# First attention: the value projection of two heads at once, in three rounded passes of 256 columns

## The reference, cut to what matters

```
q = split_heads(x @ Wq);  k = split_heads(x @ Wk);  v = split_heads(x @ Wv)
q = _apply_rope(q, cos, sin);  k = _apply_rope(k, cos, sin)
scores = einsum('bhqd,bhkd->bhqk', q, k) * scale     # causal mask, softmax
ctx = einsum('bhqk,bhkd->bhqd', attn, v)
return ctx.reshape(b, s, H * HD) @ Wo
```

## Time and profile before

| | before |
|---|---|
| median of 3 runs (1079.26 to 1084.4) | 1079.3 us |
| profiled execution: its time / its span | 1087.43 us / 1085.1 us |
| PE busy over the span | 992.0 us (91%) |
| first attention (scores of head 0 to the last mix) | 20 us to 266 us |
| DVE, ACT, POOL busy over the span | 66%, 56%, 44% |

### The profile page before, as it was taken

The page is one execution under the profiler, slowest core; times in us unless marked ns, Lnnn a source line. Parts: engine busy times, 40 slices in busy tenths (PEclk is TensorE's granted clock), DMA queues, the critical chain, the costliest instruction groups (busy, mean ns, idle before and its releaser), DMA issues. The chain is left out here.

```text
span 1085.1 us, 19309 instructions
## 1 busy us (share of the span) xinstructions
PE 992.0 (91%) x6228; PEld 822.2 (76%) x6228; DVE 720.6 (66%) x2139; ACT 606.7 (56%) x1647; POOL 480.1 (44%) x479
## 2 busy tenths in 40 slices
PE   7999999998996799849999999988878889999996
PEld 5998899887883689827888898975435568777785
DVE  5666766664587356528586757646787457888876
ACT  3656665666222355437676777637774565555553
POOL 5787668762277344354443220211237214443321
PEclk9999999999998799959999999989998999999999
DMA  6732110000011699735312121187003011112101
GB/s 216 255 122 80 30 31 27 18 15 2 1 59 56 186 345 337 258 98 180 97 60 68 50 69 40 59 135 95 21 2 118 0 59 59 59 62 78 38 1 40
DMA packets 86667, 95.60 MB, mean 88 GB/s; under 512 B 8897, under 2 KB 76295, under 8 KB 86576
## 3 DMA queue, kind: packets, MB, share of 16 engines
q1 hardware_dynamic: 82464, 85.48, 26.2%
q0 software_dynamic: 3264, 7.42, 2.2%
q10 hardware_dynamic: 848, 1.57, 0.4%
HBM read 71.22 MB, written 24.12 MB: 88 GB/s over the span
## 5 line engine op out<-in xcount | busy, mean ns | idle before, releaser
L579 POOL TENSOR_TENSOR a_qk<-h,a_by_sin 128x512 f32<-128x512 f32 x64 | 81.9, 1280 | 5.0
L278 PE MATMUL a_mix_ps<-a_probsT,a_v 128*128 128x256 f32 x256 | 78.5, 388 | 5.6 <-ACT a_probsT L310 5.6
L352 DVE CUSTOM_DVE_ANT_0 h<-a_score_ps,mask_bf 128x128 f32<-128x128 f32 (+1 forms) x128 | 40.6, 355 | 58.5 <-PE a_score_ps L345 50.3
L1298 POOL TENSOR_TENSOR a_w_l<-a_w,a_w_h 128x512 fp32r<-128x512 f32 x30 | 38.9, 1296 | 83.3 <-ACT a_w_h L1473 83.3
L358 ACT ACTIVATE y_moe<-y_moe,a_nmax 128x128 f32<-128x128 f32 x64 | 25.6, 400 | 75.8 <-DVE a_nmax L352 75.8
L339 DVE COPY a_probsT<-a_turn_ps 128x384 f32<-128x384 f32 x64 | 34.9, 546 | 48.2 <-PE a_turn_ps L269 48.2
L1025 POOL TENSOR_TENSOR e_w_l<-e_w,e_w_h 128x512 fp32r<-128x512 f32 x32 | 40.8, 1276 | 56.0 <-ACT e_w_h L1093 56.0
L459 PEld LDWEIGHTS a_proj_ps<-a_w,xT 128*128 128x128 f32 x512 | 59.6, 192 | 0.9
L80 PE MATMUL a_proj_ps<-a_x_l,a_w_h 128*128 128x512 f32 x128 | 56.8, 444 | 3.4 <-POOL a_w_l L584 3.3
L459 PE MATMUL a_proj_ps<-a_w,xT 128*128 128x128 f32 x512 | 59.7, 275 | 0.0
L2658 POOL TENSOR_TENSOR m_up_l<-m_up_w,m_up_h 128x1024 fp32r<-128x1024 f32 x8 | 19.4, 2429 | 88.8 <-ACT m_up_h L2630 88.8
(11 more groups left out here) (451 smaller groups left out, 3511.8 us busy)
## 6 DMA issues: line engine op xcount, KB each, us to landing
slots<-zeros SPq DMA_DIRECT2D x4, 2048.0 KB, 8.0
e_rows<-slots SPq DMA_DIRECT2D x32, 256.0 KB, 4.6
e_w<-in_L_ffn_w_dram SPq DMA_DIRECT2D x32, 256.0 KB, 4.8
out_slots<-e_out SPq DMA_DIRECT2D x32, 256.0 KB, 4.1
a_w<-in_L_attn_w_q_dram SPq DMA_DIRECT2D x32, 256.0 KB
e_w<-in_L_ffn_w_dram SPq DMA_DIRECT2D x32, 128.0 KB, 4.2
keys<-key_parts SPq DMA_DIRECT2D x16, 256.0 KB, 11.2
m_up_w<-in_up_dram SPq DMA_DIRECT2D x8, 512.0 KB, 3.6
```

The source lines that it names most:

```text
L278: pe.matmul(self.mix_ps[:, r, 0:S], v(0), self.probsT[:, r, 0:S], start=True, stop=False, skip_group_check=True)
L352: done = dve.tensor_tensor_reduce(self.probs[:, b, cells], self.score_ps[:, r, cells], self.k.mask_bf[:, cells], -1.0, 3e38, ALU.add, ALU. ...
L579: pool.tensor_tensor(qk[:, par, 0 if what == "q" else 1, half * HALF:(half + 1) * HALF], by_cos[:, r, :], by_sin[:, r2, :], ALU.add).then_ ...
```

## The change

v is projected for a pair of heads (2p, 2p+1) at once, by `product`. Stationary are now the high and low parts of a tile of 128 tokens of x (already there for q and k), and the 256 columns of Wv of the two heads move past them. A pair makes 4 jobs of 2 token tiles; a job is 2 tiles x 2 halves of the inner dimension x 3 passes = 12 matmuls and fills one bank. All 4 jobs of pair 0 stand ahead of the first scores; then two jobs stand in step 2 of every head up to head 13, where the two v chunks stood, and none in head 14. The value weights have a tile of their own (`w_v`, 256 KB for a pair) with a high part cut by ACT (`cut_v_high`) and a low part cut by DVE for pairs 0 and 1 (`rest_of_v`) and by POOL from pair 2 on (`cut_v_low`). Two v buffers of a pair each replace two of a head each; the buffer of the even pairs and both parts of the value weights lie where `wo` will be, so `wo` is loaded late: SP waits until head 13 is mixed. The loads of Wq and Wk of head h now wait for the low parts of head h-2, no longer for its v projection.

```diff
+        def v_job(h, c):
+            return V_JOBS * ((h + 1) // 2) + (0 if h % 2 else 2) + c - 4
+        def v_jobs(h):
+            return (4, 5) if h + 1 < H else ()
...
+                def load_v(pair):
+                    if pair:
+                        w_v_ready(sp, pair - 1)
+                    sp.dma_start(w_v[:, :, :], ...).then_inc(w_v_in, 16)
                 load_x(sp, k, I, 0)
                 load(0, 0)
                 load_x(sp, k, I, 1)
+                load_v(0)
                 load_masks(sp, k, I)
                 load(1, 1)
+                load_v(1)
                 load_rest(sp, k, I)
                 load(2, 0)
...
+                sp.wait_ge(at.mixed, B * (H - 2))
+                load_wo(sp, k, I)
...
+                def project_v(n, bank):
+                    w_v_ready(pe, n // V_JOBS)
+                    for t in range(V_TILES):
+                        tokens = slice((n % V_JOBS * V_TILES + t) * P, (n % V_JOBS * V_TILES + t + 1) * P)
+                        for kc in range(DC):
+                            last = product(pe, proj_ps[:, bank, t * 2 * HD:(t + 1) * 2 * HD],
+                                           (x_h[:, kc, tokens], x_l[:, kc, tokens]), (w_v_h[:, kc, :], w_v_l[:, kc, :]),
+                                           kc == 0, kc == DC - 1)
+                    last.then_inc(v_proj, 1)
...
-                        for t in range(NT // 2):
-                            for kc in range(DC):
-                                last = pe.matmul(proj_ps[:, c % 2, t * HD:(t + 1) * HD],
-                                                 k.xT[:, kc, half * HALF + t * P:half * HALF + (t + 1) * P],
-                                                 w[:, par, 2, kc, :], start=kc == 0, stop=kc == DC - 1)
-                        last.then_inc(v_proj, 1)
+                        project_v(v_job(h, c), c % 2)
...
+                def rest_of_v(pair):
+                    dve.wait_ge(w_v_high, pair + 1)
+                    dve.tensor_tensor(w_v_l[:, :, :], w_v[:, :, :], w_v_h[:, :, :], ALU.subtract).then_inc(w_v_first, 1)
...
                 for c in NQK:
                     rotate_in(0, c)
-
+                rest_of_v(0)
...
                             at.copy_turned(dve, n - at.TURN, (b - at.TURN) % B)
+                        if n == 1:
+                            rest_of_v(1)
                         decay(n)
...
+                    if h % 2 and h + 3 < H:
+                        cut_v_low((h + 3) // 2)
...
-                    act.wait_ge(w_in[par], 48 * (pair + 1))
-                    at_least(act, v_proj, 2 * (h - 1))
+                    act.wait_ge(w_in[par], 32 * (pair + 1))
+                    at_least(act, qk_proj, 4 * (h - 1))
...
+                        if n == 0:
+                            cut_v_high(1)
+                        if h % 2 and h + 3 < H and b == B - 1:
+                            cut_v_high((h + 3) // 2)
```

More of the change, by code:

```diff
@@ L368, in layer0_attention @@
         ROT = 4
-        w = m.sb("a0_w", [P, 2, 3, DC, HD])
+        w = m.sb("a0_w", [P, 2, 2, DC, HD])
+        w_v = m.sb("a0_w_v", [P, DC, 2 * HD])
         w_p = Parts(m, "a0_w", [P, 2, 2, DC, HD])
@@ L396, in layer0_attention, with w_v_ready @@
         NQK = {0: 1, 1: 2, 2: 3, 3: 4}
-        NV = {4: 1, 5: 2}
+        V_JOBS, V_TILES = 4, 2
+        FIRST = 2
+        def v_job(h, c):
+            return V_JOBS * ((h + 1) // 2) + (0 if h % 2 else 2) + c - 4
+        def v_jobs(h):
+            return (4, 5) if h + 1 < H else ()
+        def w_v_ready(eng, pair):
+            if pair < FIRST:
+                eng.wait_ge(w_v_first, pair + 1)
+            else:
+                eng.wait_ge(w_v_low, pair + 1 - FIRST)
         SCANS = {B * (2 + c * B + b) + B - 1: (c, b) for c in range(DC) for b in range(B)}
@@ L429, in _ @@
                     load(h, h % 2)
+                    if h % 2 and h + 1 < H:
+                        load_v((h + 1) // 2)
                     i = h - 3
@@ L436, in _ @@
                                                                        k.zeros.shape[1]])).then_inc(k.zeroed, 16)
+                sp.wait_ge(at.mixed, B * (H - 2))
+                load_wo(sp, k, I)
             @block.tensor
             def _(pe):
+                def project_v(n, bank):
[7 more added lines that the diff above has]
+                    last.then_inc(v_proj, 1)
                 def project(h, pair, par, c):
                     what, half = CHUNKS[c]
-                    if what == "v":
-                        pe.wait_ge(w_in[par], 48 * (pair + 1))
-                    else:
+                    if what != "v":
                         if h == 1:
@@ L470, in mix @@
                 def mix(h, par, b):
-                    if b % 2 == 0:
-                        pe.wait_ge(v_kept, 2 * h + b // 2 + 1)
-                    at.mix(pe, 4 * h + b, b, lambda j: v[:, par, 2 * b + j, :])
+                    pe.wait_ge(v_kept, V_JOBS * (h // 2) + b + 1)
+                    at.mix(pe, 4 * h + b, b, lambda j: v[h // 2 % 2][:, 2 * b + j, h % 2 * HD:(h % 2 + 1) * HD])
                 pe.wait_ge(k.zeros_ready, 1)
                 keep_clock(pe, proj_ps[:, 0, :], k.zeros[:, 0:P], k.zeros[:, 0:512], 2)
-                for c in range(len(CHUNKS)):
+                for c in NQK:
                     project(0, 0, 0, c)
+                for n in range(V_JOBS):
+                    if n < 2:
+                        pe.wait_ge(rot_in, NQK[n + 2])
+                    else:
+                        pe.wait_ge(v_kept, n - 1)
+                    project_v(n, n % 2)
                 pe.wait_ge(k.masks_in, 16 * MASK_LOADS)
@@ L488, in emit @@
                             for c in BESIDE[b]:
-                                project(h + 1, pair + par, 1 - par, c)
+                                if c in NQK or c in v_jobs(h + 1):
+                                    project(h + 1, pair + par, 1 - par, c)
                         if b >= at.TURN or not first:
@@ L585, in cut_low, with cut_v_low @@
                                            ).then_inc(w_low, 1)
+                def cut_v_low(pair):
+                    pool.wait_ge(w_v_high, pair + 1)
+                    pool.tensor_tensor(w_v_l[:, :, :], w_v[:, :, :], w_v_h[:, :, :], ALU.subtract).then_inc(w_v_low, 1)
                 cut_low(0, 0)
@@ L600, in _, with keep_v, cut_v_high @@
             def _(act):
[L601 to L605, removed]
+                def keep_v(n, bank):
+                    act.wait_ge(v_proj, n + 1)
+                    tiles = slice(n % V_JOBS * V_TILES, (n % V_JOBS + 1) * V_TILES)
+                    act.activation(v[n // V_JOBS % 2][:, tiles, :].rearrange("p t d -> p (t d)"), proj_ps[:, bank, :],
+                                   ACT.Copy).then_inc(v_kept, 1)
                 def cut_high(h, pair, par):
-                    act.wait_ge(w_in[par], 48 * (pair + 1))
-                    at_least(act, v_proj, 2 * (h - 1))
+                    act.wait_ge(w_in[par], 32 * (pair + 1))
+                    at_least(act, qk_proj, 4 * (h - 1))
                     for piece in range(2):
                         act.activation(w_p.h[:, par, piece], w[:, par, piece], ACT.Copy).then_inc(w_high, 1)
+                def cut_v_high(pair):
+                    act.wait_ge(w_v_in, 16 * (pair + 1))
+                    at_least(act, v_proj, V_JOBS * pair)
+                    act.activation(w_v_h[:, :, :], w_v[:, :, :], ACT.Copy).then_inc(w_v_high, 1)
                 load_turns(act, k, I)
@@ L618, in _ @@
                         cut_high(0, 0, 0)
+                cut_v_high(0)
                 cut_high(1, 0, 1)
-                for c in NV:
-                    keep_v(0, 0, c)
+                for n in range(V_JOBS):
+                    keep_v(n, n % 2)
                 def emit(h, pair, par, first, last, ahead):
```

39 lines of the change are left out of this document (23 added, 16 removed).

## The result

| | before | after |
|---|---|---|
| median of 11 runs | 1082.14 us (1079.26 to 1086.44) | 1077.08 us (1072.35 to 1081.07) |
| ratio, 95% interval | | 0.9948 (0.9927 to 0.9968) |
| profiled execution: time / span | 1087.43 / 1085.1 us | 1077.92 / 1076.0 us |

0.52% faster, with the interval (a gain of 3.5 to 7.9 us) on both sides of the 0.5% that I called the edge; -5.1 us in the medians, -5.4 were forecast. The median before is now 1082.1 and not 1079.3, since more runs were taken, so the changed kernel stands at 1077.1 instead of the 1073.9 forecast.

A forecast was written before the change was run, and what follows sets the result against it. PE, busy 225.00 of 225 us in the first attention, was taken as the bound. The terms -9.8 + 2.2 + 2.5 - 0.3 + 2.1 - 2.9 + 0.8 gave -5.4 us, a median of 1073.9 us, range 1069.5 to 1078.3.

The forecast's parts named there:

- The passes: Value projection in 14 heads: 24 fp32r passes at about 0.120 us replace 3.57 us of fp32 matmuls, -9.8 us.
- Pair 0 ahead of the first scores: Before the first scores: 48 passes instead of 32 records, 5.74 us for 3.57, +2.2 us.
- The first wait: Before pair 0's value passes: PE waits for DVE's subtraction behind the fourth rotate_in, +2.5 us (2.2 to 3.6).
- The earlier start: At the start: the first weights' high part no longer waits for Wv, -0.3 us (0 to 0.5).
- The second wait: Head 0, step 2: PE's value passes wait for DVE's subtraction for pair 1, +2.1 us (1.5 to 3.0).
- The end: Head 14, step 2 loses v's 3.57 us, but ACT then sets the pace: -2.9 us (-2.2 to -3.57).
- The clock: Behind the new waits: half a fall of the granted clock, almost all for the first, +0.8 us (0 to 3.2).
- The sum: All seven terms together: -5.4 us, 1082.0 us for an execution like the profiled one, 1073.9 for the median.
- Covered work: Cuts on ACT and POOL, the late load of wo and SP's stand lie beside other work: costed at nothing.
- The rival of the late load: Wq, Wk of head 2 after about 32 us, each us beyond adding one, or late wo: 1077 or more, chance 0.04.

The follow-up runs named there:

- fp32 pairs: Changed kernel with the value projection in plain fp32, value weights not split: 1.0041 of the kernel before; 0.9973 with SP's load of pair 1's value weights later.
- both early: Changed kernel with DVE's subtractions for pairs 0 and 1 both moved ahead of the rotate_in: 0.9909 of the kernel before, again 0.9858.
- loads first: Changed kernel with SP's load of pair 1's value weights behind the constant loads and Wq, Wk of head 2: 0.994 of the kernel before.
- late wo: Kernel before with only its wo load held until head 13 is mixed: 0.9987 of the kernel before.
- first early: Changed kernel with only DVE's subtraction for pair 0 moved ahead of the four rotate_in of head 0: 0.9922 of the kernel before.

## Why the prediction was right, step by step

- **The passes, -9.8.** Right. 13 heads in a row (scores of head 1 to those of step 2 of head 14) went from 212.40 to 203.21 us, 0.71 a head, so -9.9 for 14. The pace of 0.120 held, and the weight loads did not bind. The formula of "TensorE: Matmul & The Clock Gate" of the Trainium skill (section Back-to-back issue gap), 0.109 us for 256 columns, was not reached. The fp32 pairs show that the passes and not the pairs do it.
- **Pair 0 ahead of the first scores, +2.2.** From the first value pass to the first scores 7.31 us (20.89 to 28.20), against 3.57: +3.7, of which 1.5 is the slow clock and 2.3 the passes (5.85 us without a fall).
- **The first wait, +2.5.** 3.07, 3.07, 2.89 and 2.44 us in the four profiles that have it. I let DVE come 0.4 us before the end of a POOL operation. That is how it was in the last of the four (0.46 us before, 2.44 us of waiting); in both profiles of the changed kernel POOL had begun an operation 0.16 us before, and the whole of it had to be waited for. The cost of the blocking itself was right: in ten of ten cases in which the subtraction found POOL in an operation, it ended 0.54 to 0.56 us after that operation; three times it began just ahead of POOL, took 0.67 us, and POOL's operation took 1.8 instead of 1.3. What "SBUF — State Buffer" of the Trainium skill (section Who interferes with whom) says of a DVE operation with two SBUF inputs and a reading GpSimd operation, that the later one is blocked until the other is done, agrees with these rows. What the sum could not have was the phase, which differs from execution to execution.
- **The earlier start, -0.3.** In the first pair of profiles it did not come (PE began at 9.17, 9.04 before), but over all profiles it did: 8.91 us on average in the eight with the three passes, 9.13 in the three with the old projection, -0.2. What was not in the sum is the slow stretch behind it: from the first projection to where the value passes could start 7.4 to 7.7 us in seven profiles and 8.3 to 8.5 in the six others, all three of the old projection among the short ones. Whether the change makes the long stretch likelier or it was chance stays open; both lengths occur with the same code (both early, 7.60 and 8.32).
- **The second wait, +2.1.** 1.76 and 1.44 us in the two profiles, the one low in the range of 1.5 to 3.0, the other just under it. Again the phase: at 1.44 the subtraction came ahead of POOL's operation (0.67 us), at 1.76 it had to wait (0.99).
- **The end, -2.9.** From the scores of head 14's step 2 to the last turn 18.4 us before (245.84 to 264.21), 15.0 now (247.47 to 262.46): -3.4, nearly the whole v.
- **The clock, +0.8.** The term that was wrong by most. I took half a fall for both waits together, and expected it under 1.00 behind at most one of them. The first wait brought a fall in each of four profiles (1.5 us in three, 2.7 in the fourth), the second one in one of four (1.5): about 2.2 us on average, and in the first profile both.
- **The sum.** By the first pair of profiles, from its own terms: start +1.0, waits +3.1 and +1.8, pair 0 +3.7, middle heads -9.9, the second fall +1.5, end -3.4 make -2.2; each wait is counted from the end of the last matmul, 0.16 us behind where the next would have started, which gives -1.9, and -1.7 was measured. The second pair has -4.7; the mean of three profiles with both waits (changed twice, loads first) against three with the old projection (before twice, late wo) is -3.5. The median has -5.1, with an interval from -7.9 to -3.5, and the forecast was -5.4. So the sum had the right terms, all but the slow stretch at the start, and most of them the right size; that the number is met to 0.3 us is in part luck: the start, the first wait and the clock cost up to 4 us more than in my sum, the end and the second wait gave back about 1, and the rest lies in what the time leaves open.
- **Covered work.** The late wo, SP's stand and the cuts on ACT and POOL show no cost; each had its experiment or, for the cuts, PE's full 14.95 us in a head. wo was issued at 249.27, landed 8.2 us later and was first used at 267.57.
- **The rival of the late load** was sized at one us for each us "after about 32 us". In the fp32 pairs the load landed at 35, and PE waited 3.6 us for what follows from it; but the clock then stood at 0.50 for 7 us as well (38.5 to 45.4), and between the first scores and the first wo this kernel lost 5.9 us against the one with the loads first.

## What to carry to other kernels

When an operation that feeds the bound engine is put "behind the others" in an in-order queue, its place is worth as much as its cost: here two subtractions of together 2.6 us on DVE took 4.8 us from PE, 1.5 to 3 more through the clock, and about half of the gain; moved ahead of the rotations, where DVE was idle or early, they took nothing. When the neighbour that blocks such an operation runs back to back, give its price as a range, from no blocking to a whole operation (0 to 1.1 us were seen): the phase is not the same in every execution. And before a difference of 5 us is read from two profiles, hold the stages that the change can't reach against each other: here they differed by more.

## What the runs showed that I had not expected

The granted clock fell to 0.50 behind a wait of only 1.76 us, about 1.7 us after PE had resumed, while it held at 1.00 behind one of 1.44 us in three other executions and behind 3.2 us in the earlier trace rows. With loads first it fell before PE had even resumed, at 18.7 us in a wait of 2.89, and stayed low for 7 us.

The first 15 us differ from execution to execution of the same code: after a wait of 2.8 to 3.7 us before the first projection PE ran at half its pace for some 3 us in seven profiles and for 5 to 6 in six. In three of the six (first early, both early again, fp32 pairs) the granted clock reads 1.00 all the while, and only the spacing of the matmuls, 0.43 us for 512 columns instead of 0.23, shows it. A granted clock of 1.00 is worth a look at the pace.
